# Block 0's negated maxima inside the masked queries instead of in products of ones

## The reference, cut to what matters

```python
h = _ln(x, ln1_w, ln1_b) * (1 + sc1) + sh1
q, k, v = jnp.split(h @ Wqkv + bqkv, 3, axis=-1)
x = x + _attn(q, k, v) @ Wos + bos
h = _ln(x, ln2_w, ln2_b) * (1 + sc2) + sh2
x = x + _attn(h @ Wq + bq, context @ Wk + bk, context @ Wv + bv) @ Woc + boc
...   # then an MLP with 4 x 256 hidden, and block 1 with 16 heads of 64

def _attn(q, k, v):          # H = 16 heads of HD = 16
    scores = jnp.einsum('bhnd,bhmd->bhnm', q, k) * HD ** (-0.5)
    p = jax.nn.softmax(scores, axis=-1)
    return einsum('bhnm,bhmd->bhnd', p, v)
```

## Time and profile before

| | |
|---|---|
| median of three runs | 3895.97 us (3895.3, 3895.97, 3903.24) |
| the profiled execution | 3901.6 us, its span 3899.6 us |
| mean granted TensorE clock | 0.988 |
| TensorE busy | 3750.1 us (96% of the span) |
| VectorE busy | 2930.1 us (75%) |
| ACT busy | 1996.6 us (51%) |
| POOL busy | 2583.4 us (66%) |
| first and last transpose of maxima (L751) | 51.4 and 1046.2 us |

### The profile page before, as it was taken

One profiled execution on the slowest core, in us unless ns is written; L12 is line 12 of the kernel. 1 busy time (PEld: TensorE's weight loads), 2 busy tenths in 40 slices (PEclk: granted clock), 3 DMA queues, 4 the chain that ended last, 5 costly groups with the idle time before them and its releaser, 6 DMA issues.

```text
span 3899.6 us, 92972 instructions
## 1 busy us (share of the span) xinstructions
PE 3750.1 (96%) x34934; PEld 3217.8 (83%) x34934; DVE 2930.1 (75%) x6035; ACT 1996.6 (51%) x6534; POOL 2583.4 (66%) x2803
## 2 busy tenths in 40 slices
PE   8999999999799999999999999899999999989999
PEld 7888877777699988888888888788888888869998
DVE  6777777777655568888888888899999898974443
ACT  4555555555433335555555555555555555553333
POOL 4666655555477767666666666677777777756776
PEclk9999999999899999999999999999999999999999
DMA  2111111111111126666666667676776767772111
GB/s 83 41 35 34 47 51 50 51 50 49 53 49 49 60 70 201 221 211 214 214 217 212 215 218 227 208 233 225 231 226 222 234 221 231 228 217 69 44 44 33
DMA packets 415197, 544.98 MB, mean 140 GB/s; under 512 B 58523, under 2 KB 311965, under 8 KB 414749
## 3 DMA queue, kind: packets, MB, share of 16 engines
q1 hardware_dynamic: 267224, 404.74, 30.7%
q10 hardware_dynamic: 147524, 134.30, 12.9%
HBM read 220.11 MB, written 184.55 MB: 104 GB/s over the span
## 4 chain that ended last, share of the span: by engine, by line
PE 79%; DVE 9%; issue 4%; POOL 3%; DMA 2%; ACT 1%; ACTq 1%; SPq 0%; DVEq 0%; POOLq 0%
PE BANKS L614 19%; PE BANKS L615 17%; PE BANKS L616 17%; PE BANKS L810 6%; PE BANKS L798 6%; PE BANKS L666 3%; PE BANKS L743 2%; PE BANKS L675 2%; POOL HL L1313 2%; PE BANKS L860 2%; PE BANKS L682 1%; DMA p_scratch<-TR 1%; DVE SN L1156 1%; DMA PB<-p_scratch 1%; PE BANKS L626 1%
## 5 line engine op out<-in xcount | busy, mean ns | idle before, releaser
L962 ACT ACTIVATE PR<-BANKS,NM 128x128 f32<-128x128 f32 x2048 | 720.9, 379 | 348.3 <-DVE NM L1142 348.0
L1301 POOL TENSOR_TENSOR PR<-PR,RL 128x512 f32<-128x512 f32 x512 | 533.0, 1041 | 335.8 <-DVE RL L1108 334.9
L614 PE MATMUL BANKS<-HH,WH 128*128 128x512 f32 x1632 | 687.8, 421 | 29.6 <-POOL HL L1313 18.7
L615 PE MATMUL BANKS<-HL,WH 128*128 128x512 f32 x1632 | 643.1, 394 | 0.0
L616 PE MATMUL BANKS<-HH,WL 128*128 128x512 f32 x1632 | 642.1, 393 | 0.0
L1313 POOL TENSOR_TENSOR HL<-HF,HH 128x512 fp32r<-128x512 f32 x192 | 256.0, 1333 | 325.3 <-DVE HH L1040 163.6
L1142 DVE TENSOR_REDUCE NM<-BANKS 128x8 f32<-128x1024 f32 x256 | 310.3, 1212 | 197.2 <-PE BANKS L810 197.1
L962 ACT ACTIVATION_READ_ACCUMULATOR PR<-BANKS,NM 128x1 f32 x2048 | 444.7, 217 | 0.0
L923 ACT ACTIVATE PT<-BANKS 128x512 f32<-128x512 f32 x512 | 278.3, 596 | 279.8 <-PE BANKS L682 279.1
L614 PEld LDWEIGHTS BANKS<-HH,WH 128*128 128x128 f32 x1632 | 309.7, 190 | 122.4 <-POOL HL L1313 24.9
L614 PE MATMUL BANKS<-WH,OH 128*128 128x256 f32 x1280 | 376.0, 294 | 30.7 <-DVE OL L1160 22.7
(11 more groups left out here) (138 smaller groups left out, 10197.1 us busy)
## 6 DMA issues: line engine op xcount, KB each, us to landing
SW<-SN SPq DMA_DIRECT2D x1024, 128.0 KB, 2.8
p_scratch<-TR SPq DMA_DIRECT2D x256, 512.0 KB, 4.7
PB<-p_scratch ACTq DMA_DIRECT2D x1024, 128.0 KB, 3.6
x_scratch<-X SPq DMA_DIRECT2D x80, 512.0 KB, 3.2
X<-x_scratch SPq DMA_DIRECT2D x80, 512.0 KB, 4.6
CX<-in_ctx SPq DMA_DIRECT2D x32, 384.0 KB, 3.4
X<-in_x SPq DMA_DIRECT2D x16, 512.0 KB, 4.4
out<-X SPq DMA_DIRECT2D x16, 512.0 KB, 2.9
```

Source lines behind the costliest of these rows:

```text
L614: e.matmul(o, lh, rh, start=first and i == 0, stop=False)
L615: e.matmul(o, lh, rl, start=False, stop=False)
L962: made = e.activation(pr[:, r], bank[:, r], ACT.Exp, bias=nm[:, h:h + 1], accum_out=RL[npr(t)][:, h:h + 1])
L1301: e.tensor_tensor(p3, p3, RL[npr(t)][:, :].unsqueeze(2).broadcast_to([128, 4, 128]), ALU.mult).then_inc(s_nrm, 1)
```

## The change

It gives the negated maxima a place in rows that are zero in the masked queries. For head `e_` of a pair, the 16 rows of the other head in `QB` are zero. The maximum now sits in one of them, and the key tile has a one in the same row and zeros in the rest of that half.

- The keys become `KB[.., c, e_, ..]`, masked for each head like the queries: ACT writes two passes of 512 columns per tile instead of one (`scale` from `MASK`, `bias` from a new small `BK` that has the one in it).
- `max0` writes the negated maxima straight into `TOP`, at the columns whose transpose lands in the right rows; `top` on POOL goes away, and the split in two pieces too.
- `TOP` has 2 x 128 columns: two transposes per batch element instead of one.
- `top_out` makes `QM = top * mask + QB` in two operations of 256 elements per partition instead of one for `M`.
- `turned_scores` multiplies `KB` by `QM`, 128 columns per product, 8 of them per block instead of 4 with 256 columns; `turned_tops`, `SEL` and `M` are gone.
- `v_out` is one operation of 8 x 32 columns. For that the two heads of a pair stand side by side in `V`, the ones around them, and the readers of the sums and values (`sums`, `scale0`) take the other half than before.
- The first MLP's activation waits for the end of the turned scores, as its buffers share memory with the new tiles.

```diff
-                for stage, lag in (("v", -3), ("v_out", -2), ("top", 4), ("top_turn", 5), ("top_out", 5), ("pv0", 10), ("sums", 11), ("scale0", 12),
+                for stage, lag in (("v", -3), ("v_out", -2), ("top_turn", 5), ("top_out", 5), ("pv0", 10), ("sums", 11), ("scale0", 12),
...
+        BK = sb("BK", [128, 2, 2, 2])
...
-            KF = [sb(f"KF{i}", [128, 2, 512], stack=first) for i in range(2)]
-            sb("HOLE0", [128, 7 * 512], stack=first)
-            M = [sb(f"M{i}", [128, 2, 128], R, stack=first) for i in range(2)]
-            SEL = sb("SEL", [128, 2, 128], R, stack=first)
-            TOP = [sb(f"TOP{i}", [128, 4, 32], R, stack=first) for i in range(2)]
+            KB = [sb(f"KB{i}", [128, 2, 2, 512], stack=first) for i in range(2)]
+            sb("HOLE0", [128, 2 * 512], stack=first)
+            QM = [sb(f"QM{i}", [128, 2, 2, 128], stack=first) for i in range(2)]
+            TOP = [sb(f"TOP{i}", [128, 2, 128], stack=first) for i in range(2)]
...
-                    made = e.matmul(PS[r % 2][:, 256 * c + 128 * e_:256 * c + 128 * e_ + 128], QB[ga % 2][rows, c, e_, s], KF[ga % 2][rows, c, s],
-                                    start=True, stop=True)
+                    made = e.matmul(PS[r % 2][:, 128 * k:128 * k + 128], QB[ga % 2][rows, c, e_, s], KB[ga % 2][rows, c, e_, s], start=True, stop=True)
...
-                    e.matmul(PS[2 + r % 2][:, 256 * c:256 * c + 256].rearrange("p (e n) -> p e n", e=2), KF[ga % 2][rows, c, s], QB[ga % 2][rows, c, :, s],
-                             start=c == 0, stop=False)
-
-            def turned_tops(y, c):
...
-                    made = e.matmul(PS[2 + r % 2][:, 256 * c:256 * c + 256].rearrange("p (e n) -> p e n", e=2), SEL[rows, c, :], M[y.i // 2 % 2][rows, :, :],
-                                    start=False, stop=c == 1)
+                    made = e.matmul(PS[2 + r % 2][:, 128 * k:128 * k + 128], KB[ga % 2][rows, c, e_, s], QM[y.i // 2 % 2][rows, c, e_, :], start=True, stop=True)
...
-                    q.wait_ge(s_topl, vi + 1)
+                    q.wait_ge(s_nm0, 2 * vi + 2)
                     q.wait_ge(*tp.free(("top", x)))
-                    e.transpose(PS[tp.bank(("top", x))][:, 0:128], TOP[vi % 2][:, :, :].bitcast(F).rearrange("p r n -> p (r n)"), ID[:, :]).then_inc(s_tt, 1)
+                    for c in range(2):
+                        made = e.transpose(PS[tp.bank(("top", x))][:, 128 * c:128 * c + 128], TOP[vi % 2][:, c, :], ID[:, :])
+                    made.then_inc(s_tt, 1)
...
-                    e.activation(KF[ga % 2][:, j, :], PS[tp.bank(("k", p, g, j))][:, :], ACT.Identity,
-                                 bias=col("bk", j) if p else col("bqk", 2 + j)).then_inc(s_kf, 1)
+                    for e_ in range(2):
+                        made = e.activation(KB[ga % 2][:, j, e_, :], PS[tp.bank(("k", p, g, j))][:, :], ACT.Identity, bias=BK[:, p, j, e_:e_ + 1],
+                                            scale=MASK[:, 2 + e_:3 + e_])
+                    made.then_inc(s_kb, 1)
...
-                    q.wait_ge(s_topl, x.i // 2 - 1)
-                    e.tensor_reduce(NM0[x.i // 2 % 2][:, x.h, :, :], BANKS[:, 0:2, :].rearrange("p r (h k) -> p r h k", h=4), AX, ALU.max,
-                                    negate=True).then_inc(s_nm0, 1)
+                    q.wait_ge(s_tt, x.i // 2 - 1)
+                    q.wait_ge(s_const, 2)
+                    top = TOP[x.i // 2 % 2][:, :, 64 * x.h:64 * x.h + 64].rearrange("p c (r k n) -> p r c k n", r=2, k=2)[:, :, :, :, 0]
+                    e.tensor_reduce(top, BANKS[:, 0:2, :].rearrange("p r (c k n) -> p r c k n", c=2, k=2), AX, ALU.max, negate=True).then_inc(s_nm0, 1)
...
-                    e.tensor_tensor(M[vi % 2][:, :, :], PS[tp.bank(("top", x))][:, 0:128].unsqueeze(1).broadcast_to([128, 2, 128]),
-                                    MASK[:, 2:4].unsqueeze(2).broadcast_to([128, 2, 128]), ALU.mult).then_inc(s_m, 1)
+                    ga, s = xq(x.p, x.g), slice(128 * x.b, 128 * x.b + 128)
+                    for e_ in range(2):
+                        made = e.scalar_tensor_tensor(QM[vi % 2][:, :, e_, :], PS[tp.bank(("top", x))][:, 0:256].rearrange("p (c n) -> p c n", c=2),
+                                                      MASK[:, 4 + e_:5 + e_], QB[ga % 2][:, :, e_, s], ALU.mult, ALU.add)
+                    made.then_inc(s_m, 1)
...
-                    for e_ in range(2):
-                        o = V[vi % NV][:, :].rearrange("p (i r) -> p i r", r=64)[:, :, 48 * e_:48 * e_ + 16]
-                        made = e.tensor_tensor(o, bank[:, 0:D].rearrange("p (i e d) -> p i e d", e=2, d=16)[:, :, e_, :],
-                                               TB[:, 2 * x.p + 1, :].rearrange("p (i e d) -> p i e d", e=2, d=16)[:, :, e_, :], ALU.add)
-                    made.then_inc(s_vd, 1)
+                    e.tensor_tensor(V[vi % NV][:, :].rearrange("p (i r) -> p i r", r=64)[:, :, 16:48], bank[:, 0:D].rearrange("p (i d) -> p i d", d=32),
+                                    TB[:, 2 * x.p + 1, :].rearrange("p (i d) -> p i d", d=32), ALU.add).then_inc(s_vd, 1)
```

More of the change, by code:

```diff
@@ L258, in build @@
         NM = [sb(f"NM{i}", [128, 8]) for i in range(2)]
-        NM0 = [sb(f"NM0_{i}", [128, 2, 2, 4]) for i in range(2)]
         RC = [sb(f"RC{i}", [128, 2, 2, 4]) for i in range(2)]
@@ L339, in build @@
         s_win = [sem(f"win{i}") for i in range(NSTG)]
-        s_pro_t, s_col, s_silu, s_sil, s_slt, s_mod_mm, s_mod, s_mods, s_half, s_vone, s_const, s_bq, s_sel = (
-            sem(k) for k in ("pro_t", "col", "silu", "sil", "slt", "mod_mm", "mod", "mods", "half", "vone", "const", "bq", "sel"))
+        s_pro_t, s_col, s_silu, s_sil, s_slt, s_mod_mm, s_mod, s_mods, s_half, s_vone, s_const, s_bq = (
+            sem(k) for k in ("pro_t", "col", "silu", "sil", "slt", "mod_mm", "mod", "mods", "half", "vone", "const", "bq"))
         s_whi, s_wlo = sem("whi"), sem("wlo")
@@ L348, in build @@
         s_bias, s_res = sem("bias"), sem("res")
-        s_q, s_qb, s_k, s_kf, s_v, s_vd = (sem(k) for k in ("q", "qb", "k", "kf", "v", "vd"))
-        s_s0, s_nm0, s_toph, s_topl, s_tt, s_m, s_ts, s_to, s_rc, s_no, s_of = (
-            sem(k) for k in ("s0", "nm0", "toph", "topl", "tt", "m", "ts", "to", "rc", "no", "of"))
+        s_q, s_qb, s_k, s_kb, s_v, s_vd = (sem(k) for k in ("q", "qb", "k", "kb", "v", "vd"))
+        s_s0, s_nm0, s_tt, s_m, s_ts, s_to, s_rc, s_no, s_of = (
+            sem(k) for k in ("s0", "nm0", "tt", "m", "ts", "to", "rc", "no", "of"))
         s_s, s_nm, s_exp, s_rl, s_nrm, s_pv0, s_pv = (sem(k) for k in ("s", "nm", "exp", "rl", "nrm", "pv0", "pv"))
@@ L435, in build @@
             for p, g, j in at["k", tick]:
[L436 removed]
+                tp.add(("k", p, g, j), FOUR, s_kb, 2 * xq(p, g) + j + 1)
             for x in at["v", tick]:
@@ L719, in _ @@
                 for c in range(2):
[L720 to L732, removed]
+                    for e_ in range(2):
+                        for x in halves:
+                            made = scores(x, c, e_)
+                            if c == e_ == 1:
+                                made.then_inc(s_s0, 1)
+                        for y in turned:
+                            made = turned_scores(y, c, e_)
+                            if c == e_ == 1:
+                                made.then_inc(s_ts, 1)
                 for x in at["pv0", tick]:
@@ L1088, in _ @@
                     for e_ in range(2):
-                        made = e.reciprocal(RC[vi % 2][:, :, e_, :], TO[vi % 2][:, :, e_, :, 16 - 16 * e_])
+                        made = e.reciprocal(RC[vi % 2][:, :, e_, :], TO[vi % 2][:, :, e_, :, 16 * e_])
                     made.then_inc(s_rc, 1)
@@ L1268, in _ @@
             for top in TOP:
-                e.memset(top[:, :, :].bitcast(F), 0.0).then_inc(s_const, 1)
+                e.memset(top[:, :, :], 0.0).then_inc(s_const, 1)
             for tick in ticks:
-                for x in at["top", tick]:
-                    vi = 4 * xq(x.p, x.g) + x.b
-                    nm, top = NM0[vi % 2][:, :, :, :].rearrange("p h r n -> p (h r) n"), TOP[vi % 2]
-                    q.wait_ge(s_const, 2)
-                    q.wait_ge(s_nm0, 2 * vi + 2)
-                    q.wait_ge(s_tt, vi - 1)
-                    e.tensor_copy(top[:, :, 0:4], nm).then_inc(s_toph, 1)
-                    q.wait_ge(s_toph, vi + 1)
-                    e.tensor_tensor(top[:, :, 4:8], nm, top[:, :, 0:4].bitcast(F), ALU.subtract).then_inc(s_topl, 1)
                 for x in at["scale0", tick]:
@@ L1378, in _constants @@
     row = np.arange(128)[:, None] % 32
-    mask = np.concatenate([0.25 * (row // 16 == np.arange(2)), (row < 8) & (row % 2 == np.arange(2)), (row < 8) & (row % 4 // 2 == np.arange(2))],
-                          axis=1).astype(f)
+    own = row // 16 == np.arange(2)
+    mask = np.concatenate([0.25 * own, own, row == 16 * (1 - np.arange(2))], axis=1).astype(f)
```

25 lines of the change are left out of this document (13 added, 12 removed).

## The result

The changed kernel took **3920.1 us** (median of four runs, 3918.72 to 3925.05), the kernel before 3897.66 in the same comparison (3895.3 to 3903.24). The ratio is **1.0056, interval [1.0043, 1.0068]**: slower by some 22 us, more than the 0.2% that can be told from no change. The time is inside the range of 3866 to 3922; the forecast, no change, was wrong. The profiled execution took 3918.72 us for a span of 3916.8 (3899.6 before).

The account below looks back on a forecast made before the run. TensorE bounds most blocks, with M ready only some 0.1 us earlier; VectorE's chain sets group ends. Terms gave 16 x 0.00 - 16 x 0.05 = -0.8 us, about -1 from the median 3895.97: 3895 us, range 3866 to 3922.

Parts of the forecast that it names:

- Products of maxima leave: TensorE's blocks: without the four L682 products a TensorE-bound block takes 0.22 us less, 1.08 instead of 1.30.
- A second transpose: TensorE, per batch element: two transposes of maxima last 0.38 us against 0.27 for one, so M starts 0.11 later.
- Value bias: VectorE: two operations of 128 elements become one of 256, about 0.05 us less, counting only where VectorE is the chain.
- keys written twice: ACT: a second key pass, +0.75 us twice per group, covered by waits and costed at nothing.
- Rival A: All blocks: QM is hidden and TensorE sets the time; -1.32 us per group, 3854 us; chance 0.15.
- Rival C: ACT becomes the wait: half the extra key pass (0.4 us) shows in each group; +13 us, 3908 us; chance 0.07.
- Rival D: TensorE's turned products: weight loads bound the narrower products; +165 us and more, about 4060 us; chance 0.03.
- M becomes QM: VectorE, between transposes and block: one operation becomes a pair lasting 0.75 us, +0.33, bounds +0.16 and +0.42.
- The sum for the first stage: Block 0's self-attention: five blocks -1.10, transposes +0.11 and +0.66, group's end +0.33; 0.00 us per group.
- The sum for the second stage: Block 0's cross-attention: savings in TensorE-bound blocks against QM in VectorE's chain and HF's wait; -0.05 us per group.
- Rival B: First stage: longer waits at group ends bring its clock below 1.00; +26 us, 3922 us; chance 0.13.
- POOL loses two small operations: POOL, per batch element: they lie in the wait for VectorE's maxima, so removing them gains nothing.

Follow-up runs that it names:

- e2: Kernel before without the products of maxima, M still made, nothing subtracted, exponent scaled by 0.01: 3863.79 us, ratio 0.9903.
- e6: Changed kernel with the value bias as two operations again: 3919.63 us, ratio 1.006.
- e4: Kernel before with each key tile written twice by ACT, first into a buffer nobody reads: 3899.86 us, ratio 0.9998.
- e1: Changed kernel with the transposes of the maxima one tick earlier, ahead of the block, and QM ahead of the next maximum: 3841.41 us, ratio 0.9843.
- e7: Kernel before with its transpose of maxima one tick earlier, ahead of the block, and M a tick earlier: 3985.49 us, ratio 1.0232.
- e9: Changed kernel with the transposes of maxima and QM one tick earlier, but the transposes behind the block: 3944.57 us, ratio 1.0116.
- e5: Changed kernel with QM's two halves signalled one by one and the block's products ordered head by head: 3894.83 us, ratio 0.9997.
- e3: Kernel before with M made twice, first into a buffer that nobody reads: 3935.09 us, ratio 1.0085.

## Why the prediction was right and wrong

Right, with their numbers:

- *Products of maxima leave*: 0.21 less per block (forecast 0.22). It counts in five blocks of eight in the first stage, as forecast, and e2's -1.1 us per group fits that.
- *A second transpose*: the pair lasts 0.38, and it adds 0.11 to the way to QM. *Value bias* (e6) and *keys written twice* (e4): nothing.
- *QM gates blocks*: two or three blocks in four batch elements wait for it (30 waits in 10 groups, 27 in some 14).
- Rival A (TensorE sets the time) is refuted: its busy time fell and the time rose. Rival C by e4, run on the kernel before. Rival D by the block of 1.10 us, 0.11 per record of a row strip as in the scores before. The Trainium skill, "TensorE: Matmul & The Clock Gate", section "The mechanism", would have a load wait for the product of its own row group; in this trace it does not add to the time.

Wrong:

- **The term "M becomes QM" was mis-sized.** The pair lasts 0.87 to 0.88 us, not 0.75: I took L1136's 407 ns, where one operation takes 478, and their distance is 0.40 instead of 0.34. The step that failed is the inference from L1031, 0.29 us for 128 elements against 277 ns for an addition, that the kind of operation costs nothing. It was of another shape, and its operands are both in SBUF. The extra VectorE time is +0.46, above the range's end of +0.42 (which itself should read 2 x 0.407 - 0.41 = +0.40). Each QM wait has that in it: +0.47 to 0.49 from transposes to block instead of +0.33.
- **The sum for the first stage, 0.00, is +0.47.** Its structure was right, term by term: five blocks -1.05 (forecast -1.10), one pair of transposes +0.10 (+0.11), the group's end +0.42 (+0.33), and the two blocks behind v +0.96 (+0.66). "What TensorE saves there is absorbed in waits" holds at the group's end. The mis-sized QM is in the last two terms, and most of the miss is in the two blocks behind v.
- **The sum for the second stage, -0.05, is +0.97.** Some 0.6 of it is waits: HF's is 1.98 where 1.8 was forecast, and two blocks wait for QM where the forecast had one. In a group with the low clock of each kernel (from 786.85 before, from 769.64 now) both start 1.39 us behind their transposes where it was 0.84, +0.55 each; the forecast had +0.33 for one and +0.11 for the other. Another 0.3 is a case that I had placed in the wrong stage. Rival B had the first stage fall to the low clock, and the first stage kept 1.00. I read one group of the second stage as the pattern of all, and so held it to be at its floor already. In fact 5 of 13 groups escaped the low clock; now 2 do. The view that would have told is the distance of the stores over many groups, some 31.9 or 33.2. The mean of 0.97 says it too: four us at 0.58 are 1.7 us of clock lost in a group of 32.7, and in every group that would be a mean of 0.95.
- **"POOL loses two small operations: Nothing"** holds for the order as it stands, and missed what that removal makes possible: e1 against e7 is 144 us between two kernels with the same early order.

Still open: why 7 us come back behind the two stages; 0.08 us of the second stage's +0.97; and what decides whether a group falls to the low clock. HF's wait alone does not: at 1.09 us no group falls in e1, and 12 of 13 do in e9, where TensorE waits 1.2 us more for X; at 1.45 us 8 of 13 do (before); at 1.98 us 11 of 13 in the changed kernel and 8 of 13 in e5.

## What to carry to other kernels

Work taken from the engine that is 95% busy is worth nothing where that engine waits for a chain, and a lengthened chain is charged at every wait that hangs on it, not only at the first. Count these waits in each stage by itself. When a step has become longer, look for the place where its engine has nothing to do (here: while the block runs that the next maximum must wait for) and put it there: the same kernel went from 1.0056 to 0.9843 of the time before. And price a group from many groups: one that is looked at may be one of two kinds.

## What the runs showed of the hardware

- A multiply-add of a PSUM and an SBUF tensor, with a column of SBUF as its scalar, takes 477 ns for 256 elements, and 0.88 us for two, so 0.40 from start to start; an addition of the same shape and memories takes 407 to 410.
- A record whose profile names "issue" as what it waited for can be waiting for a semaphore: in e3 one of a group's three waits of the same line is named after M, and in e5 the 12.2 us of such waits in the first stage go when the signal comes earlier.
- The low clock comes in a share of otherwise equal groups: before the change 8 of 13 have it, while HF's wait is 1.45 to 1.49 us in all 13. TensorE's longest wait doesn't fix the share: it is 11 of 13 at 1.98 us in the changed kernel and 8 of 13 at 1.98 us in e5.
